# A scratch tile of 64 columns in place of 256 between GpSimd's indirect transfers

## The reference

```python
x = x + attn_a(layernorm(x))
x = x + ffn(layernorm(x))
x = x + attn_b(layernorm(x))
x = x + ffn(layernorm(x))

def ffn(x):                                   # 4096 tokens
    shared = silu(x @ sg_w.T) * (x @ su_w.T) @ sd_w.T
    probs = sigmoid(x @ router_w.T + routing_bias)
    topk_p, topk_idx = top_k(probs, 2)        # 2 of 8 experts, weights normed to sum 1
    ...
    return shared + sum over both choices of weight * expert(x)
```

## Time and profile before

| | us |
|---|---|
| median of 3 runs | 1026.67 |
| lowest and highest run | 1026.3, 1032.23 |
| the profiled execution | 1028.98 |
| its span, first to last instruction | 1027.1 |
| PE busy in the span | 819.4 |
| DVE busy | 735.8 |
| POOL busy | 586.9 |
| ACT busy | 568.5 |

### The profile page before, as it was taken

One profiled execution on the slowest core, in us unless ns is written; L12 is line 12 of the kernel. 1 busy time (PEld: TensorE's weight loads), 2 busy tenths in 40 slices (PEclk: granted clock), 3 DMA queues, 4 the chain that ended last, 5 costly groups with the idle time before them and its releaser, 6 DMA issues. The chain is left out here.

```text
span 1027.1 us, 19542 instructions
## 1 busy us (share of the span) xinstructions
PE 819.4 (80%) x6459; PEld 545.3 (53%) x6459; DVE 735.8 (72%) x1506; ACT 568.5 (55%) x805; POOL 586.9 (57%) x815
## 2 busy tenths in 40 slices
PE   3887577899986787888888888979796588899890
PEld 2666566799984333333333333333342256799890
DVE  3888745455563658899999998989789646555574
ACT  1454152133334667989898989998763242233230
POOL 2343486881383666666644444455326877788884
PEclk9999588999997878999999999999877688999996
DMA  9990012123338477584737474732210021132444
GB/s 273 300 131 1 16 39 70 54 81 114 101 84 242 124 197 220 150 227 118 234 108 215 116 208 121 224 106 55 70 42 24 32 75 39 40 102 84 132 135 122
DMA packets 114401, 124.00 MB, mean 121 GB/s; under 512 B 13328, under 2 KB 76560, under 8 KB 114176
## 3 DMA queue, kind: packets, MB, share of 16 engines
q1 hardware_dynamic: 96512, 100.80, 36.2%
q0 software_dynamic: 8416, 17.29, 5.4%
q10 hardware_dynamic: 9376, 4.65, 1.6%
HBM read 59.97 MB, written 62.72 MB: 119 GB/s over the span
## 5 line engine op out<-in xcount | busy, mean ns | idle before, releaser
L2070 DVE TENSOR_SCALAR ring_b<-psum 128x1024 int32<-128x1024 int32 x160 | 194.2, 1216 | 24.0 <-PE psum L1765 20.8
L1930 ACT ACTIVATE ring_a<-psum 128x1024 f32<-128x1024 f32 x160 | 162.4, 1021 | 51.0 <-PE psum L1765 45.7
L1936 ACT ACTIVATE ring_b<-ring_b 128x1024 f32<-128x1024 f32 x160 | 168.7, 1055 | 36.5 <-DVE ring_b L2070 36.1
L2198 POOL TENSOR_SCALAR_AFFINE_SELECT ring_b<-ring_b 128x512 f32<-128x512 f32 (+1 forms) x112 | 80.1, 728 | 171.6 <-ACT ring_b L1936 170.9
L1765 PE MATMUL psum<-stacks 32*128 32x128 f32 (+3 forms) x1024 | 98.9, 385 | 66.2 <-DVE ring_b L2070 36.8
L1765 PEld LDWEIGHTS psum<-stacks 32*128 32x128 f32 x1024 | 56.9, 193 | 173.5 <-ACT ring_a L1930 76.6
L2062 DVE TENSOR_SCALAR ring_a<-ring_a 128x1024 f32<-128x1024 f32 x160 | 119.4, 751 | 16.8 <-ACT ring_a L1930 15.0
L949 ACT ACTIVATE ring_b<-psum 128x512 f32<-128x512 f32 x72 | 42.6, 591 | 114.0 <-PE psum L834 88.0
L1818 PE MATMUL psum<-ring_b,values 128*32 128x256 f32 (+3 forms) x1024 | 94.2, 478 | 8.6 <-POOL ring_b L2198 8.6
L1797 PE MATMUL psum<-ring_a,ones_s 128*32 128x256 f32 (+3 forms) x1024 | 92.3, 469 | 9.8 <-POOL ring_a L2198 9.8
L1092 POOL DMA_INDIRECT r_rows<-y_sorted,rows_of x64 | 67.1, 1048 | 51.3 <-DMA y_sorted<-y_out 39.2
(11 more groups left out here) (220 smaller groups left out, 1484.1 us busy)
## 6 DMA issues: line engine op xcount, KB each, us to landing
stack_q<-parts SPq DMA_DIRECT2D x32, 256.0 KB
stack_ky<-parts SPq DMA_DIRECT2D x32, 256.0 KB
stacks<-stack_q SPq DMA_DIRECT2D x64, 128.0 KB
stacks<-stack_ky SPq DMA_DIRECT2D x64, 128.0 KB
stack_k<-parts SPq DMA_DIRECT2D x32, 256.0 KB
stacks<-stack_k SPq DMA_DIRECT2D x64, 128.0 KB
stack_qr<-parts SPq DMA_DIRECT2D x32, 256.0 KB
stacks<-stack_qr SPq DMA_DIRECT2D x64, 128.0 KB
```

What stands on the lines that cost most here:

```text
L1930: nc.scalar.activation(exps[:, n % RING, 2 * u:2 * u + 2, :], psum[:, first:first + 2, :], ACT.Exp, scale=SCALE).then_inc(self.exp, 1)
L1936: nc.scalar.activation(part, part, ACT.Ln, bias=1.0).then_inc(self.ln, 1)
L2070: nc.vector.tensor_scalar(ring[:, m % RING, HEADS_B[u][0]:HEADS_B[u][1] + 1, :].bitcast(I32), psum[:, first:first + 2, :].bitcast(I32), 0x ...
L2198: ins = nc.gpsimd.affine_select(out=part, in_=part, pattern=[[0, part.ap[1][1]], [1, 128]], compare_op=ALU.is_ge, fill=0.0, base=0, channe ...
```

## The change

The scratch tile of `pause` gets 64 columns in place of 256. The write after an indirect DMA has a quarter of the columns; its number, its place and the wait behind it stay. One line serves both expert stages.

```diff
--- before.py
+++ after.py
@@ -484,7 +484,7 @@
                 if ffn_1.first_late + k <= B:
                     ffn_1.pool_rstd(p, ffn_1.first_late + k)
 
-        pause_room, paused, pauses = sb("pause_room", [128, 256]), sem("paused"), [0]
+        pause_room, paused, pauses = sb("pause_room", [128, 64]), sem("paused"), [0]
 
         def pause(p):
```

## The result

| | before | changed |
|---|---|---|
| median, us | 1029.45 | 1056.55 |
| lowest and highest of 4 runs | 1026.3, 1036.28 | 1053.6, 1060.61 |
| span of the profiled execution | 1027.1 | 1057.3 |

The changed kernel takes 1.0253 times as long (95% interval 1.0211 to 1.0296). Forecast were 1014.2 us and a range of 1009 to 1026: the sign is wrong and the range missed. (The forecast counted from 1026.67, the median of three runs; with a fourth it is 1029.45, which changes nothing in the sign.)

The account below looks back on a forecast made before the run. POOL was taken to set the end, its late scatters holding up PE in the last expert stage. Gains of 9.7 + 1.0 + 1.0 + 0.8 = 12.5 us from 1026.67 gave 1014.2 us, range 1009 to 1026.

Parts of the forecast that it names:

- The price of the pause: Scratch write after each indirect transfer: 0.16 us at 64 columns, 0.165 saved per pause, a POOL step of 1.40.
- Paid back: Rival: the wait moves into the next transfer, so 0.035 us per pause is left; 1023 us, chance 0.19.
- The small terms: Gains outside the last stage: end of attention 1.0 us, first expert stage 1.0, fetches 0.8.
- The last mask: End of attention: PE waits 6.16 us for POOL's mask, which comes earlier with shorter pauses; 1.0 us gained.
- ScalarE's 0.42 for the bias of batch 8: First expert stage: a wait behind POOL's sends that shorter pauses cover; lower bound of that stage's 1.0 us gain.
- DVE's 1.71 for the second batch: Fetches: DVE's wait for the second batch's fetch, then PE 1.10 for DVE; shorter pauses gain 0.8 us.
- sends that end sooner: Before the first scatter: 37 sends shorten by 6.1 us, more than the 2.7 lost there; POOL then waits for quad 0.
- The last stage, the largest term: Last expert stage: POOL's quad falls from 6.62 to 5.96 us, PE sets the pace, last scatter 9.7 us earlier.
- quads beyond 6.3: Sign: if short pauses work but PE's quads stretch beyond 6.3 us, the last stage's term is wrong.
- The pause protects something: Rival: long runs of quick transfers make transfers longer as descriptors pile up; 1060 us with all at 1452 ns, chance 0.09.
- the bare scatters at the end: Last three scatters, without pauses between, start 1.27 us apart with 0.96 us transfers; cited against transfers getting longer.
- DVE's copies: Rival: in the last stage each transfer meets and waits for a DVE weight copy (L1468); 1046 us, chance 0.04.

Follow-up runs that it names:

- the kernel with one row: The kernel before with each pause writing 256 columns of one partition in place of 128 partitions; 1024.34 us, ratio 0.9924.
- the two versions that were to gain: Kernel before with 64 columns in last-stage sends: 1028.68 us; or 192 in first sends, 256 in fetches, 64 in last sends, 192 in scatters: 1026.43 us.

## Why the prediction was wrong, step by step

**The price of the pause: right.** 0.16 and a step of 1.40 were forecast; 0.17 and 1.41 came. "Paid back" falls with it: a transfer behind a short pause takes 0.96 and starts 0.28 behind it.

**The small terms: right in kind.** The last mask came earlier: PE's wait for it went from 6.16 to 4.77, 1.4 where 1.0 was forecast. ScalarE's 0.42 for the bias of batch 8 is gone, its start at 141.51 where it was 142.92. DVE's 1.71 for the second batch is 0.80. In the stretch before the first scatter the forecast had 1.0 for the mask and 2.4 for sends that end sooner; 7.2 came, but in the two runs with 64 columns in the last sends alone and in the last stage alone it is 117.2 and 117.1 us long, where three kernels with 256 columns there have 118.3 to 120.7, so only 1 to 3.6 of the 7.2 recur. The changed kernel's timelines of PE, ScalarE and DVE:

```profile
845.44 1.93 PE L1818 MATMUL psum<-ring_b,values 128*32 128x512 f32 x8 [4.77 <-POOL ring_b L2198]
```

```profile
141.51 1.65 ACT L918 ACTIVATE r_rows<-x_res,f_nbias,f_rstd 128x128 f32<-128x128 f32 x4
```

```profile
323.19 2.31 DVE L1491 SCALAR_TENSOR_TENSOR x_res<-r_rows,gate,x_res 128x128 f32<-128x128 f32 x8 [0.80 <-DMA r_rows<-y_sorted,rows_of]
```

Each of these gains was real where it stood. The stretch from the first send to the first fetch then lost 15.7 and the fetch 10, for which the forecast had gains of 1.0 and 0.8.

**The last stage, the largest term: the first half right, the second wrong.** POOL did drop out. ScalarE's four waits for y_token, 10.5 us, are gone: the list of waits of the scatter stage has none, and PE's own waits and late signals stand in their place:

```profile
ACT ring_b L949 <- PE psum L834: 47.3, 20, 3.8
...
ACT ring_b L949 <- remote: 12.6, 4, 3.9
...
ACT ring_a L956 <- remote: 6.2, 3, 2.3
```

The sum then let PE run at 6.16 to 6.25 a quad. ScalarE's timeline, some of the quads emptied:

```profile
933.45 0.59 ACT L965 COPY y_out<-psum 128x512 f32<-128x512 f32 x1
...
968.64 0.59 ACT L965 COPY y_out<-psum 128x512 f32<-128x512 f32 x1
...
977.01 0.60 ACT L965 COPY y_out<-psum 128x512 f32<-128x512 f32 x1
...
983.09 0.59 ACT L965 COPY y_out<-psum 128x512 f32<-128x512 f32 x1
...
1033.77 0.59 ACT L965 COPY y_out<-psum 128x512 f32<-128x512 f32 x1 [0.90 <-PE psum L848]
```

From quad 2 to quad 16 are 100.3 us for 14 quads, 7.17 each: slower than the 6.62 that POOL had set before. The quads fall into two kinds: 977.01 to 983.09 is 6.08, the forecast pace and better; 968.64 to 977.01 is 8.37, and in it stand three signals late by 3.05 to 3.38 us. So the failed step is the one that took PE's own pace as something that the pause does not touch: from the first scatter to the last it gave 107.9 us (896.2 to 1004.1), and 121.1 came. The prediction had named this sign itself, quads beyond 6.3. The same step cost far more in the first expert stage, where the sum let the pages run at PE's pace and counted gains: of the 30 us by which the profiled execution grew, 26 went there, and with 64 columns in that stage alone the kernel takes 1.0215 times as long, where the change takes 1.0253. The term for signals held back stood in no part of the sum. The quads without a late signal ran as the sum had it. With a step of 1.54 nearly all do: the kernel with one row empties its quads 6.07 to 6.69 apart up to quad 15 and is 0.8% faster than before.

**The rivals.** "The pause protects something" was the right side and had the right place, long runs of quick transfers, and its 1060 us happens to lie near the result, which is luck. Its mechanism was wrong: it looked for POOL's transfers to get longer, and their median is 966 ns where it was 963:

```profile
L1071 POOL DMA_INDIRECT y_token<-y_out,token_of x71: 959/966/1349, 922.4 to 1043.5; - x71
```

What the pause protects is another engine's signals. So the argument against it, that the bare scatters at the end show no lengthening, was no evidence: by then PE has nothing left to signal (its last matmul ends at 1004.6, the bare scatters start at 1012.5). With 0.09 it was given too little for what was known, since the trace had no run of transfers at 1.41. "DVE's copies" is far too small: L1468's median is 427 ns, where it was 428, and the late signals are not DVE's. A little of it is there all the same, which the prediction did not see: the scatter of 1452 ns starts at 992.88, while DVE copies in L1468 (992.74 to 993.49), and of the changed kernel's 199 sends and scatters the 48 that meet such a copy take 1053 ns on average, the other 151 take 978: under 4 us in all.

Was there a trace of it beforehand? A faint one, which the waits don't show, since nobody was waiting. During the attention POOL issues single fetches without a pause, and in the kernel before seven of PE's signals there are 0.13 to 0.40 us late, each landing 1.29 to 1.37 us after the start of such a fetch. Whoever had compared signal records with matmul ends would have had a reason to give that rival more.

## What to carry to other kernels

A wait that seems to do nothing may protect an engine that does not appear in it; before shortening it, look at what the others send and receive while it runs, not only at the engine that holds it. In a trace, a wait that ends with "remote" on a single core, or an engine that starts microseconds after its producer ended, says to compare the records of signals with the ends of instructions. Where GpSimd issues indirect transfers in a row beside matmuls, try the spacing as a size of its own: here, against the 1.57 us from start to start of before, 1.54 gained 0.5 to 0.8%, 1.41 lost 2.5% and 1.26 8%.

## What the runs showed of the hardware that was not expected

Runs of indirect transfers of GpSimd hold back the semaphore signals of TensorE, and not those of VectorE, ScalarE or GpSimd itself (0.012 us at most): up to 9.0 us at 1.41 us from start to start, 22.7 at 1.26, against 0.015 in quiet stretches. The Trainium skill, page "Perfetto Trace Analysis", section on the TensorE instruction, says that the recorded end of a matmul is an estimate, and that its signal leaves only when PSUM has acknowledged the last bytes. This agrees with a signal that can be late with no instruction being long, which these traces show; whether the acknowledgement or the way of the signal is held up, no run here shows, nor whether it is the making of the descriptors or the transfer's own writes that hold it.

When a signal is held, and when it gets through, is partly to be seen from where it falls behind the start of the last transfer. In the changed kernel 30 of the 89 signals whose matmul ended 0.8 to 1.4 us after such a start are over 0.3 us late, 18 of 96 before 0.8, 4 of 15 between 1.4 and 1.6, and none of 95 from 1.6 to 3.0; in the kernel before it is 4 of 58, 1 of 115, 0 of 25 and 0 of 87. At steps of 1.54 and 1.51, 30 of 34 late signals land 1.25 to 1.5 us after a start, before the next transfer or just as it begins; in the changed kernel, where the next start comes at 1.41, 14 of 52 do. In five of the seven kernels with steps of 1.41 (all but the two versions that were to gain) 103 of 194 late signals land at 1.3 to 1.6 and 36 at 0.6 to 0.8. This fits a signal that is let through about 1.3 us after the last start and is held again when the next transfer comes first, but no run here shows what holds it. Why most signals of the first 0.8 us pass at once, while one that is held waits for several transfers, stays open; so does why the last stage's sends have signals late by 0.7 us at most where all their steps are 1.41, in four kernels, and by 1.8 and 2.8 where long steps stand between.

The landing of an indirect transfer did not change. The last scatter of the changed kernel and SP's load behind it:

```profile
1043.52 0.96 POOL L1071 DMA_INDIRECT y_token<-y_out,token_of  x1 [0.30 <-issue]
1045.80 2.02 SPq L1086 DMA_DIRECT2D r_rows<-y_token  x4
```

From the scatter's start to the load that waits for its landing are 2.28 us, 2.27 before. The fixed cost of about 2.0 us that the Trainium skill gives such a transfer (page "DMA: Bandwidth & Descriptors", section on the anatomy of one DMA) agrees in size, and it is paid side by side: the starts come down to 1.26 apart.
